# A cross-attention kernel on one core: two raw places for K's right sides, and GpSimd sums in the first batches

## What is computed

```python
memory_proj = jnp.einsum('bme,de->bmd', memory, W_mem)
scores = jnp.einsum('bnd,bmd->bnm', hidden_states, memory_proj) / jnp.sqrt(jnp.float32(D))
attn = jax.nn.softmax(scores, axis=-1)
memory_context = jnp.einsum('bnm,bmd->bnd', attn, memory_proj)
gate_input = jnp.concatenate([hidden_states, memory_context], axis=-1)
gate = jax.nn.sigmoid(jnp.einsum('bnf,df->bnd', gate_input, W_gate) + b_gate)
fused = hidden_states + gate * memory_context
return _rmsnorm(fused, norm_w)
```

## Time and profile before

| | |
|---|---|
| median of 3 runs | 932.72 us (932.04 to 935.44) |
| the profiled execution's own time | 932.3 us |
| its span | 930.6 us |
| TensorE busy | 910.1 us, 98% |
| VectorE busy | 751.0 us, 81% |
| ScalarE busy | 420.6 us, 45% |
| GpSimd busy | 54.4 us, 6% |
| mean granted TensorE clock | 0.995 |

### The profile page before, as it was taken

One profiled execution on the slowest core, in us unless ns is written; L12 is line 12 of the kernel. 1 busy time (PEld: TensorE's weight loads), 2 busy tenths in 40 slices (PEclk: granted clock), 3 DMA queues, 4 the chain that ended last, 5 costly groups with the idle time before them and its releaser, 6 DMA issues.

```text
span 930.6 us, 11736 instructions
## 1 busy us (share of the span) xinstructions
PE 910.1 (98%) x4376; PEld 765.6 (82%) x4376; DVE 751.0 (81%) x961; ACT 420.6 (45%) x624; POOL 54.4 (6%) x73
## 2 busy tenths in 40 slices
PE   9899999999999999998899999999999999999996
PEld 7778888888888888887678888888888888888885
DVE  5996667767767988779497589888889888988887
ACT  4432222322232454454445355555555655555553
POOL 0000000000000000000000011011111111111002
PEclk9999999999999999999999999999999999999999
DMA  9314255556444665785759935555555554445542
GB/s 339 132 38 148 91 181 204 199 208 221 187 164 144 240 220 196 256 278 190 277 204 361 394 106 201 204 204 203 197 189 179 181 170 178 170 173 195 204 180 91
DMA packets 54680, 183.74 MB, mean 197 GB/s; under 512 B 5600, under 2 KB 11488, under 8 KB 48864
## 3 DMA queue, kind: packets, MB, share of 16 engines
q1 hardware_dynamic: 54336, 182.47, 55.0%
q10 hardware_dynamic: 288, 0.52, 0.2%
HBM read 127.93 MB, written 55.05 MB: 197 GB/s over the span
## 4 chain that ended last, share of the span: by engine, by line
PE 91%; DMA 5%; DVE 1%; SPq 1%; issue 1%; ACT 1%; POOL 0%; DVEq 0%; ACTq 0%
PE psum L1524 30%; PE psum L1525 30%; PE psum L1526 30%; DMA r_a_raw<-in_xr 2%; DMA wb_high_spill<-wp_h 1%; DMA wb_low_spill<-wp_l 1%; PE psum L1623 1%; DMA wp_other<-y_spill 1%; DMA wp_raw<-y_spill 0%; DVE wp_raw L1139 0%; ACT wp_h L639 0%; SPq L418 0%; SPq L402 0%; SPq L365 0%; ACT zb L892 0%
## 5 line engine op out<-in xcount | busy, mean ns | idle before, releaser
L1524 PE MATMUL psum<-g1h,xh 128*128 128x512 f32 x416 | 162.1, 390 | 3.5 <-DVE zr L1043 3.2
L1525 PE MATMUL psum<-g_l,xh 128*128 128x512 f32 x416 | 161.9, 389 | 0.0
L1524 PEld LDWEIGHTS psum<-g1h,xh 128*128 128x128 f32 x416 | 78.1, 188 | 20.9 <-issue 4.1
L1525 PEld LDWEIGHTS psum<-g_l,xh 128*128 128x128 f32 x416 | 78.1, 188 | 16.2
L1399 DVE TENSOR_TENSOR zb<-psum,zb 128x512 f32<-128x512 f32 x112 | 76.8, 686 | 16.1 <-PE psum L1526 16.1
L1526 PE MATMUL psum<-g1h,xs_l 128*128 128x512 f32 x192 | 74.7, 389 | 0.0
L639 ACT ACTIVATE xh<-xs_raw 128x512 fp32r<-128x512 f32 x48 | 30.3, 632 | 95.7 <-PE psum L1526 95.7
L614 POOL TENSOR_TENSOR stat<-stat 128x1 f32<-128x1 f32 x30 | 19.8, 660 | 857.6 <-ACT zb L880 857.6
L1524 PE MATMUL psum<-yh,ws_h 128*128 128x512 f32 x160 | 62.4, 390 | 0.0
L1526 PE MATMUL psum<-yh,ws_l 128*128 128x512 f32 x160 | 62.3, 389 | 0.0
L1120 DVE TENSOR_TENSOR z<-psum,bias 128x512 f32<-128x512 f32 x48 | 33.2, 691 | 30.6 <-PE psum L1526 30.5
(11 more groups left out here) (198 smaller groups left out, 2508.6 us busy)
## 6 DMA issues: line engine op xcount, KB each, us to landing
b_raw<-in_xt SPq DMA_DIRECT2D x32, 512.0 KB, 7.6
zb<-z_spill SPq DMA_DIRECT2D x16, 1024.0 KB, 6.9
xrow<-in_x SPq DMA_DIRECT2D x30, 512.0 KB, 6.4
out<-xrow SPq DMA_DIRECT2D x30, 512.0 KB, 3.9
xs_raw<-in_xt SPq DMA_DIRECT2D x12, 1024.0 KB, 4.9
z_spill<-z SPq DMA_DIRECT2D x12, 1024.0 KB, 8.3
y_spill<-y SPq DMA_DIRECT2D x40, 256.0 KB, 4.4
yt_raw<-y_spill SPq DMA_DIRECT2D x16, 512.0 KB, 3.6
```

Source lines behind the costliest of these rows:

```text
L1524: nc.tensor.matmul(tile, ah, mh, start=start, stop=False, skip_group_check=True)
L1525: nc.tensor.matmul(tile, ah, ml, start=False, stop=False, skip_group_check=True)
```

## The change

Four things change.

1. K's right sides have two raw places (185 and 177 KB), used in turn (`wp_place`), and a semaphore for each. `load_wp(n)` waits for block n - 2, and in SP's queue the loads stand earlier: those of n = 6 and 7 between the activation loads of super-batch 1, n = 8 behind `store_y(1, 2)`, n = 9 between the activation loads of super-batch 2, n = 10 behind `store_y(2, 3)`, n = 11 in super-batch 3. `store_wp` of product 6's block stands ahead of the last four activation loads. ScalarE waits for the store of n - 1, since the high place is still one. Some `load_wb_low` move to super-batches 2 to 4.
2. In the first four batches GpSimd makes T2, T3, S3, T4 and the second half (batches 2, 3) of S1. VectorE keeps T1, the first half of S1, S2 and S4.
3. A21 and A22 come as two pairs of halves (batches 0, 1 and batches 2, 3), and B11's second slice is loaded from ScalarE's queue.
4. VectorE takes stage 1's outputs, between S1's slices, ahead of stage 0's.

```diff
-        WP_AT = [(A21_AT, A21_AT + 4, 201), (185, 157, 109)]
+        WP_RAW_AT = [A21_AT, 185, 177]
...
+        def wp_place(n):
+            return 0 if n < N_WT else 1 + n % 2
...
-            sp.dma_start(r_a21[:, :, :, :], xr[2]).then_inc(r21_in, DMA)
-            sp.dma_start(r_a22[:, :, :, :], xr[3]).then_inc(r22_in, DMA)
+            for h in range(2):
+                js = slice(2 * h, 2 * h + 2)
+                sp.dma_start(r_a21[:, :, js, :], xr[2][:, :, js, :]).then_inc(r21_in[h], DMA)
+                sp.dma_start(r_a22[:, :, js, :], xr[3][:, :, js, :]).then_inc(r22_in[h], DMA)
...
             def load_wp(n):
                 m, i = wp_blocks[n]
-                if n >= 1:
+                if m == 0 and n >= 1:
                     sp.wait_ge(wp_stored, DMA * wp_stores_by[n - 1])
+                elif n >= N_WT + 2:
+                    if wp_direct(n - 2):
+                        sp.wait_ge(wp_low, n - 1)
+                    else:
+                        sp.wait_ge(wp_stored, DMA * wp_stores_by[n - 2])
+                    if len(WP_FROM[i]) > 1:
+                        sp.wait_ge(wp_sum, wp_sums_by[n - 1])
...
                 load_x_block(s + 1, 0, 1)
                 load_x_block(s + 1, 1, 1)
+                if s == 1:
+                    sp.wait_ge(ws_sum, 4)
+                    sp.wait_ge(ws_low, WS_CUT[S1])
+                    load_wp(K_AT[1, 3])
+                    load_wp(K_AT[1, 6])
+                elif s >= 2:
+                    store_wp(K_AT[s - 1, 6])
+                    if s == 2:
+                        load_wp(K_AT[2, 6])
                 sp.wait_ge(y_mm, 2 * P7 * s + 2)
                 load_x_block(s + 1, 0, 0)
                 sp.wait_ge(y_mm, 2 * P7 * s + 4)
                 load_x_block(s + 1, 1, 0)
-                if s == 1:
-                    sp.wait_ge(ws_sum, 4)
-                    sp.wait_ge(ws_low, WS_CUT[S1])
-                elif s >= 2:
-                    store_wp(K_AT[s - 1, 6])
-                if s >= 1:
-                    load_wp(K_AT[s, 3])
                 store_y(s, 0)
-                if s == 1:
-                    for i in (1, 2):
-                        load_wb_low(i, 0)
-                elif s == 2:
-                    k_quarter_stored(0, 0)
+                if s == 2:
+                    load_wb_low(1, 0)
...
                 if s >= 1:
                     store_wp(K_AT[s, 3])
-                    load_wp(K_AT[s, 6])
+                if s == 3:
+                    load_wp(K_AT[3, 6])
                 store_y(s, 2)
+                if s == 1:
+                    load_wp(K_AT[2, 3])
                 store_y(s, 3)
+                if s == 2:
+                    load_wp(K_AT[3, 3])
...
+            pool.wait_ge(r21_in[1], DMA)
+            pool.wait_ge(r22_in[1], DMA)
+            pool.tensor_tensor(r_s1[:, :, 2:4, :], r_a21[:, :, 2:4, :], r_a22[:, :, 2:4, :], ALU.add).then_inc(pool_sum, 1)
+            pool.wait_ge(g1_b22_in, DMA)
+            pool.wait_ge(g1_sum, 1)
+            pool.tensor_tensor(t2_made[:, :, :], g1_raw[B22][:, :, :], g1_raw[T2][:, :, :], ALU.subtract
+                               ).then_inc(pool_sum, 1)
+            pool.tensor_tensor(g1_raw[T3][:, :, :], g1_raw[B22][:, :, :], g1_raw[T3][:, :, :], ALU.subtract
+                               ).then_inc(pool_sum, 1)
+            pool.wait_ge(r_sum, R_SUM[S1])
+            pool.wait_ge(pool_sum, P_SUM[S1])
+            pool.tensor_tensor(r_a21[:, :, :, :], r_a11[:, :, :, :], r_a21[:, :, :, :], ALU.subtract).then_inc(pool_sum, 1)
+            pool.wait_ge(g1_low, G1_CUT[1])
+            pool.wait_ge(pool_sum, P_SUM["T2"])
+            pool.tensor_tensor(g1_raw[T4][:, :, :], g1_raw[T4][:, :, :], t2_made[:, :, :], ALU.subtract
+                               ).then_inc(pool_sum, 1)
...
             def wp_cut_high(n):
                 m, i = wp_blocks[n]
-                act.wait_ge(wp_in, DMA * wp_loads_by[n])
+                act.wait_ge(wp_in[wp_place(n)], DMA * wp_loads(n))
                 if WP_SUMS[i]:
                     act.wait_ge(wp_sum, wp_sums_by[n])
+                if n > N_WT:
+                    act.wait_ge(wp_stored, DMA * wp_stores_by[n - 1])
...
+            g1_t1()
+            r_sums(S1)
+            g1_cut(T1)
+            for j in range(NR):
+                r_out(1, j)
+                r_cut(2, j)
             for j in range(NR):
                 r_out(0, j)
-            for stage in range(2, P7):
+            for stage in range(3, P7):
```

More of the change, by code:

```diff
@@ L109, in build @@
                for j in range(NR)] for c in range(3)]
-        WP_AT = [(A21_AT, A21_AT + 4, 201), (185, 157, 109)]
[L114 to L117, removed]
+        WP_RAW_AT = [A21_AT, 185, 177]
+        wp_raws, wp_ls = zip(*[raw_low(f"wp{n}", [PART, 2, BANK], kb) for n, kb in enumerate(WP_RAW_AT)])
+        wp_other = [at(f"wp{m}_other", [PART, 2, BANK], F32, (A21_AT + 4, 157)[m]) for m in range(2)]
+        wp_h = [at(f"wp{m}_h", [PART, 2, BANK], F32R, (201, 109)[m]) for m in range(2)]
+        wp_third = [at(f"wp{m}_third", [PART, 2, BANK], F32, (201, 169)[m]) for m in range(2)]
         b11_raw, b11_l = raw_low("b11", [PART, 2, 4, N], A21_AT)
@@ L183, in build @@
         r12_in, g1_b21_in = [sem(f"r12_{h}_in") for h in range(2)], [sem(f"g1_b21_{h}_in") for h in range(2)]
[L184 removed]
+        g1_b12_in, g1_b22_in = sem("g1_b12_in"), sem("g1_b22_in")
+        r21_in, r22_in = [sem(f"r21_{h}_in") for h in range(2)], [sem(f"r22_{h}_in") for h in range(2)]
         bias_in = sem("bias_in")
         ident_done = sem("ident_done")
[L187 removed]
+        g1_sum, g1_first_high, pool_sum = sem("g1_sum"), sem("g1_first_high"), sem("pool_sum")
         g1_high, g1_low = sem("g1_high"), sem("g1_low")
@@ L206, in build @@
         y_stored = [sem(f"y{i}_stored") for i in range(Y_SLOTS)]
-        wp_in, wp_sum, wp_high, wp_low, wp_stored = (sem("wp_in"), sem("wp_sum"), sem("wp_high"), sem("wp_low"),
+        wp_in, wp_sum, wp_high, wp_low, wp_stored = ([sem(f"wp{n}_in") for n in range(3)], sem("wp_sum"), sem("wp_high"), sem("wp_low"),
                                                      sem("wp_stored"))
@@ L295, in build, with wp_raw, wp_loads @@
         wp_stores_by = list(accumulate(1 if wp_direct(n) else 2 for n in range(N_WP)))
+        def wp_place(n):
+            return 0 if n < N_WT else 1 + n % 2
+        def wp_raw(n):
+            return wp_raws[wp_place(n)]
+        def wp_loads(n):
+            return sum(len(WP_FROM[i]) * (1, 2)[m] for k, (m, i) in enumerate(wp_blocks[:n + 1])
+                       if wp_place(k) == wp_place(n))
         def wp_source(n):
             m, i = wp_blocks[n]
-            return (wp_other[m] if i == T2 else wp_raw[m])[:, :, :]
+            return (wp_other[m] if i == T2 else wp_raw(n))[:, :, :]
         def gx_banks(b):
@@ L683, in r_cut_high @@
                 if i == 6:
-                    act.wait_ge(r22_in, DMA)
+                    act.wait_ge(r22_in[j // 2], DMA)
+                elif i == S3 or (i == S1 and j >= 2):
+                    act.wait_ge(pool_sum, P_SUM[i])
                 else:
@@ L1033, in r_out @@
                 dve.wait_ge(gx_mm, NR * stage + j + 1)
-                if stage == 0:
+                if i == 1:
                     dve.wait_ge(bias_in, DMA)
@@ L1037, in r_out @@
                     dve.wait_ge(zr_first, DMA * NR)
-                dst, more = {0: (first, bias[:, HALF[0]]), 1: (first, None), 3: (c22, bias[:, HALF[1]]),
+                dst, more = {0: (first, None), 1: (first, bias[:, HALF[0]]), 3: (c22, bias[:, HALF[1]]),
                              2: (c12, bias[:, HALF[1]]), 5: (c12, None), 4: (c22, None), 6: (first, bias[:, HALF[0]])}[i]
                 if more is None:
-                    dve.wait_ge(gx_z, NR * {1: 0, 5: 3, 4: 2}[i] + j + 1)
+                    dve.wait_ge(gx_z, NR * {0: 0, 5: 3, 4: 2}[i] + j + 1)
                     more = dst
@@ L1131, in wp_sums @@
                 m = wp_blocks[n][0]
-                raw, other, third = wp_raw[m][:, :, :], wp_other[m][:, :, :], wp_third[m][:, :, :]
-                dve.wait_ge(wp_in, DMA * wp_loads_by[n])
+                raw, other, third = wp_raw(n)[:, :, :], wp_other[m][:, :, :], wp_third[m][:, :, :]
+                dve.wait_ge(wp_in[wp_place(n)], DMA * wp_loads(n))
                 if j == 1:
```

85 lines of the change are left out of this document (35 added, 50 removed).

## The result

The changed kernel takes 936.4 us (median of 7 runs, 935.37 to 938.52); the kernel before, run beside it, takes 933.94 us (7 runs, 932.04 to 935.44). The ratio is 1.0036, 95% interval 1.002 to 1.0052: the change made the kernel slower by 0.4%, little, but clear of the noise. The profiled execution took 935.37 us, so its span of 933.6 us stands 3.0 us above the span of before, where the forecast had 3.3 (935.6 against 932.3).

What follows compares the result with a forecast made beforehand. TensorE, busy 98% of the 930.6 us span, was taken as the bound, so only its waits and lower clock could pay. 932.3 - 10.7 (K's right sides) + 14.0 (start) = 935.6, forecast 935, range 916 to 941 for 8 in 10.

Steps and rivals of the forecast that it cites:

- K part: TensorE's waits at 419 and 462 us go (7.2 us), with the clock drops behind them (3.5 us): -10.7 us.
- margin of 0.2 us: Slack at VectorE's addition before TensorE's next product, read from super-batch 1 and assumed for the other two super-batches.
- The covers of the queue: Loads moved past others in SP's queue still land before their readers; activation loads of super-batch 2 covered by 3 us.
- Rival 4: K's right sides: a store or load still ends last, one or both waits stay, +4.5 to +10.7 us; chance 0.07 with blocking.
- Turns with full blocking: First four batches: GpSimd's sums and VectorE's two-SBUF-input instructions wait for each other's whole length; start +14.0 us, total 935; chance 0.50.
- GpSimd's price: First four batches: one GpSimd sum of 2048 elements, counted as three streams, takes 4.7 us.
- The clock: After TensorE stands for 7 us before S2's stage, one drop of its clock adds 1.7 us.
- The sum: Whole kernel: 932.3 - 10.7 + 14.0 = 935.6 us, forecast as 935.
- No disturbance: First four batches: GpSimd and VectorE don't disturb each other, TensorE goes on at 28.0; 917.9 us; chance 0.25.
- GpSimd keeps its turn: First four batches: GpSimd runs its queued sums in succession while VectorE's slice waits; start +18.2, total 939.8 us; chance 0.10.
- Partly blocked: First four batches: only part is blocked, or GpSimd needs 1.6 to 3 us a sum; 921 to 928 us; chance 0.08.
- the prize: Start: TensorE would go on at 28.0 instead of 31.45, a gain of 3.4 us, and 0.3 us more at 65.0.

Runs made afterwards that it cites:

- fills: Changed kernel with GpSimd's five sums replaced by fills with zero of the same tiles, sums left out: 920.99 us, ratio 0.9868.
- copies: Changed kernel with GpSimd's five sums replaced by copies of their first input, sums left out: 925.37 us, ratio 0.9915.
- the start alone: Kernel before with only the changes in the first four batches, K's right sides as before: 948.29 us, ratio 1.0157.
- late outputs: Changed kernel with all sums on VectorE and the outputs of stages 0, 2 and 3 taken a stage later: 921.84 us, ratio 0.9879.
- the K part alone: Kernel before with only the changed treatment of K's right sides (two raw places, earlier loads): 922.96 us, ratio 0.989.

## Why the prediction was right, step by step

**K part, -10.7: right.** Alone it measured -10.35. In spans it is -10.1 (930.6 to 920.5), of which S1's stage, 0.4 us later in that execution (31.85 against 31.45), takes 0.4: -10.5 for the part itself. Both waits went and both drops of the clock with them. The load of T4 is issued at 396.1, which is 383 and some 13 us that the start had lost by then (VectorE's cut of 378.85 is at 392.4 here), and VectorE's subtraction of it starts at 426.55 without a wait. What I read off super-batch 1 at the addition repeats too, but it is not a margin of 0.2 us. VectorE in super-batch 2 of the changed kernel, as the earlier trace rows, then TensorE:

```profile
430.73 1.23 DVE L1003 TENSOR_TENSOR wp_l<-wp_raw,wp_h 128x1024 fp32r<-128x1024 f32 x1 [2.96 <-ACT wp_h L693]
431.87 0.68 DVE L1262 TENSOR_TENSOR y<-psum,y 128x512 f32<-128x512 f32 x1
```

```profile
432.36 0.39 PE L1572 MATMUL psum<-yh,ws_l 128*128 128x512 f32 x1
432.70 0.47 PE L1570 MATMUL psum<-yh,w_h 128*128 128x512 f32 x1
```

The addition ends at 432.55, and TensorE's next product starts at 432.70, 0.34 us behind the matmul ahead of it where the pace is 0.23. In super-batch 1 of the kernel before the same step is 0.34 us as well (380.48 to 380.82), also 0.15 us behind the addition's end, and no other product between 340 and 419 us starts late. So nothing was to spare at that place in either kernel: the addition most likely comes 0.1 us late, too little to show as a wait.

The covers of the queue held: no reader of a moved load waits. Rival 4 falls. One of them was closer than I reckoned. The eight loads of 256 KB in super-batch 1 take 8.0 us of SP's queue (376.0 to 384.0), not 4, so the activation loads behind them go out some 4 us later than forecast. The first pair has landed by 392.8 and ScalarE reads it at 394.5: 1.7 us were left of the 3.

**Turns with full blocking: right, in the direction that no row of before showed.** It was read from one-element additions waiting for VectorE, and turned round by argument; the slice of 4.46 us shows it, and fills against copies show that the reading does it. Step by step: GpSimd's half of S1 to 30.28 (forecast 28.65); S1's stage from 30.94 (29.35); slices ending at 35.82 and 40.81 (34.55, 39.85); T4 to 50.23 (49.85); S2's sum to 52.38 (52.05); first slice from 54.50 (54.25); TensorE at 55.28 (54.95). The shift of 1.6 us at the first step has its cause ahead of it. The forecast had T1 begin at 19.8, as soon as stage 0's outputs no longer stand before it, and its low part end at 26.1. In the trace T1 begins at 21.47, since the low part before it waits for ScalarE and that for TensorE, which was later in this execution, and T1's low part ends at 28.03; GpSimd's half of S1 waits for it. The shift shrank to 0.3 us because a sum takes 4.4 us and not 4.7: four whole sums give back 1.2. Two small errors cancelled there, so it is luck that TensorE's start came within 0.3 us.

**GpSimd's price, 4.7 us: right in size, wrong in form.** I had put one, two and three streams at 1.6, 3.1 and 4.7 us. The runs show 1.8 us for the fill, 1.8 for the copy and 4.4 for the sum. The first input costs nothing beside the output, the second costs 2.6 us. GPSIMD Engine Reference of the Trainium skill, Performance versus the Vector engine, has 4497 ns for the sum, and the trace agrees within 0.1 us: 4.4 us a whole sum, and 30.28 - 28.03 = 2.25 us for the 1024 columns of half of S1.

**The clock, +1.7: nearly.** Behind the 6.4 us wait 7 matmuls start in 2.72 us where 12 would, and 58 to 61 has 0.92: 5 x 0.228 + 0.24 = 1.4 us. The drop inside S1's stage (0.66 over 41 to 46) was hidden, as forecast: it only shortened the gap ahead of the fourth piece from 1.96 to 0.36 us.

**The sum.** 12.8 (55.28 - 42.45; the forecast had 42.35) + 1.4 - 0.3 (the gap at 65.0 is gone) - 10.5 = +3.4 us, against 3.0 between the spans. The 0.4 us are not assigned. As a change the forecast was +3.3 us, against +2.5 between the medians. The forecast of 935, rounded down from 935.6, lies 1.4 us below the median of 936.4, since it was added to a profiled execution of before that was 1.6 us below its own median of 7 runs.

**The rivals.** No disturbance (917.9): what GpSimd would have to do for it is shown by the fills, whose profiled span of 917.1 is 13.5 us below before, against the 14.4 worked out. GpSimd keeps its turn (939.8): it never does, a slice gets in behind every sum; but the start alone shows a case halfway, where GpSimd gets one more sum in ahead of the first slice. Partly blocked (921 to 928) fits none of the whole sums.

**The missed step: the prize.** I put the start's prize at 3.4 us (TensorE going on at 28.0). Where S1's stage goes on without a gap it begins at 28.96 (all sums on VectorE), 29.48 (fills) and 29.76 (late outputs): 1.7 to 2.5 us, not 3.4, as stage 1 itself ends later in these. It does so in the K part alone too (its last matmul starts at 29.58 against 27.91, with this part of the program as before), so much of what is missing comes from the executions and not from the change. And with all sums on VectorE the next stage takes even that back: S2's first slice is at 42.54, against 41.42 before, and that kernel is above the K part alone (925.31, 922.96). I had followed the gain to the first stage and not to the one behind it. It did not touch the forecast, since blocking swallowed the prize anyway.

## What to carry to other kernels

Before giving work to an idle engine beside a busy one, look in the trace for any place where both have run together on SBUF operands, however small, and read the longest against the shortest instance of the same operation; where they take turns, an instruction handed over can cost the other engine its full length, here 4.4 us for 2.2 us of work saved, and cutting it up mostly changed who waits. Follow a gain to the next stage that depends on the same engine. And time the parts of a change apart: this one held -10.4 us and +15.0 us, and together they showed as +2.5.

## What the runs showed of the hardware that I had not expected

- GpSimd's fill and its copy of 128x2048 float32 take the same 1.8 us, its addition of two inputs 4.4 us.
- The same wait of TensorE can cost its clock or not. After 3.2 us of standing still the stretch behind it had 1.00 in the kernel before; after 3.3 us, with VectorE making all sums, it had 0.50 for at least 5.7 us; after 3.2 us, with the copies, it had 0.59 from 48 to 51 us. What tells the two apart was not settled.
- TensorE's first matmuls of stage 0 start at 5.1 us in the profiled execution of before and at 5.25 in that of the kernel with B11's slice back on SP's queue, and between 5.9 and 6.5 in all the others, the K part alone among them (6.2, where this part of the program is as before). So about a microsecond of the start differs between executions, and no edit here is shown to explain it.
